# Sums' reciprocals spread by DMA and divided on GpSimd, a third norm by pairs of blocks with token-major scores, and combine weights turned eight tiles at once

## What is computed

```python
x = x + 0.5 * ffn(layernorm(x), ...)
x = x + attn(layernorm(x), ...)
x = x + 0.5 * ffn(layernorm(x), ...)
```

## Time and profile before

| | us |
|---|---|
| three runs | 1883.06, 1894.16, 1893.02 |
| median | 1893.02 |
| profiled execution | 1892.63 |
| its span | 1890.8 |
| mean granted TensorE clock | 0.965 of full |

### The profile page before, as it was taken

One profiled execution on the slowest core, in us unless ns is written; L12 is line 12 of the kernel. 1 busy time (PEld: TensorE's weight loads), 2 busy tenths in 40 slices (PEclk: granted clock), 3 DMA queues, 4 the chain that ended last, 5 costly groups with the idle time before them and its releaser, 6 DMA issues.

```text
span 1890.8 us, 38698 instructions
## 1 busy us (share of the span) xinstructions
PE 1764.9 (93%) x14955; PEld 754.2 (40%) x14955; DVE 1623.5 (86%) x1980; ACT 1468.3 (78%) x2741; POOL 371.9 (20%) x547
## 2 busy tenths in 40 slices
PE   5699998879999999999999999999999999699998
PEld 3488776712222222222222222222222223377786
DVE  6566775689999999999999999999999994476665
ACT  3455564719999999999999999999999996346455
POOL 4366551300000000000000000000000000155565
PEclk9899997859999999999999999999999998899999
DMA  4454330220000100000010000001000010523542
GB/s 117 93 129 125 105 105 1 100 85 9 32 20 22 33 24 21 26 32 20 22 34 23 22 26 31 20 22 35 22 22 27 30 28 3 107 91 111 104 137 78
DMA packets 66415, 98.90 MB, mean 52 GB/s; under 512 B 12091, under 2 KB 33408, under 8 KB 66212
## 3 DMA queue, kind: packets, MB, share of 16 engines
q1 hardware_dynamic: 62070, 94.32, 17.9%
q10 hardware_dynamic: 4160, 2.10, 0.4%
HBM read 84.94 MB, written 11.04 MB: 51 GB/s over the span
## 4 chain that ended last, share of the span: by engine, by line
PE 43%; ACT 27%; issue 4%; DVE 4%; DMA 1%; POOL 1%; SPq 0%; POOLq 0%; ACTq 0%; DVEq 0%
ACT at_prob L1158 26%; PE ps L1233 16%; PE ps L1221 15%; PE ps L615 3%; PE ps L633 3%; PE ps L623 3%; DVE at_mx L1268 2%; ACT at_sums L1163 1%; POOL e_part L688 1%; DMA e_cw<-comb_rows 1%; PE ps L1197 1%; PE ps L1354 0%; DVE ps L701 0%; PE ps L1369 0%; PE ps L1442 0%
## 5 line engine op out<-in xcount | busy, mean ns | idle before, releaser
L1268 DVE TENSOR_REDUCE at_mx<-ps 128x1 f32<-128x1024 f32 x1024 | 1169.4, 1216 | 12.4 <-PE ps L1197 12.4
L1158 ACT ACTIVATE at_prob<-ps 128x512 f32<-128x512 f32 x2048 | 1111.0, 595 | 71.9 <-PE ps L1221 51.8
L1233 PE MATMUL ps<-at_prob,vals 128*32 128x256 f32 x8192 | 656.3, 392 | 15.2 <-ACT at_sums L1163 15.2
L1197 PE MATMUL ps<-k_head,q_head 48*128 48x512 bf16 x2048 | 641.3, 389 | 12.1 <-PEq L801 7.8
L1221 PE MATMUL ps<-q_head,k_head 51*128 51x512 bf16 x2048 | 630.9, 383 | 4.9
L1233 PEld LDWEIGHTS ps<-at_prob,vals 128*32 128x32 f32 x8192 | 162.3, 108 | 430.1 <-ACT at_prob L1158 405.1
L688 POOL TENSOR_TENSOR e_part<-e_silu,e_cw 128x512 f32<-128x512 f32 (+1 forms) x208 | 268.0, 1289 | 269.5 <-ACT e_silu L659 122.9
L1221 PEld LDWEIGHTS ps<-q_head,k_head 51*128 51x128 bf16 x2048 | 130.1, 93 | 434.8 <-ACT at_prob L1158 402.9
L701 DVE TENSOR_TENSOR ps<-e_part,ps 128x512 f32<-128x512 f32 (+1 forms) x208 | 144.6, 695 | 155.9 <-POOL e_part L688 155.2
L659 ACT ACTIVATE e_silu<-ps 128x512 f32<-128x512 f32 (+1 forms) x208 | 124.4, 598 | 142.0 <-PE ps L615 140.1
L1092 POOL TENSOR_TENSOR at_mparts<-at_neg,at_zero 128x8 bf16<-128x8 f32 x64 | 12.9, 202 | 1104.9 <-DVE at_neg L1276 1104.9
(11 more groups left out here) (255 smaller groups left out, 1242.7 us busy)
## 6 DMA issues: line engine op xcount, KB each, us to landing
e_cw<-comb_rows SPq DMA_DIRECT2D x80, 256.0 KB, 3.3
e_cw<-comb_rows SPq DMA_DIRECT2D x32, 224.0 KB, 3.0
e_cw<-comb_rows SPq DMA_DIRECT2D x32, 192.0 KB, 3.1
q_head<-q_rows SPq DMA_DIRECT2D x64, 96.0 KB
k_head<-k_rows SPq DMA_DIRECT2D x64, 96.0 KB
e_cw<-comb_rows SPq DMA_DIRECT2D x32, 160.0 KB, 2.9
e_cw<-comb_rows SPq DMA_DIRECT2D x48, 96.0 KB, 2.8
e_cw<-comb_rows SPq DMA_DIRECT2D x32, 128.0 KB, 3.0
```

Source lines behind the costliest of these rows:

```text
L1158: act.activation(prob[:, t % PROBS, c, :], ps[:, S + n % SRING, :], ACT.Exp).then_inc(exped, 1)
L1197: made = pe.matmul(ps[:, M + 2 * (r % MRING) + one, :], q[h % BUFS][HALF:HALF + KR, tile * P:(tile + 1) * P], k[h % BUFS][HALF:HALF + KR, ...
L1233: done_one = pe.matmul(ps[32 * j:32 * j + 32, O, half * HALF_BLK:(half + 1) * HALF_BLK], vals[h % BUFS][:, g, :], prob[:, t % PROBS, j // ...
L1268: dve.tensor_reduce(mx[u % BUFS][:, j // 2, j % 2:j % 2 + 1], ps[:, at:at + 2, :].rearrange("p a t -> p (a t)"), AX.X, ALU.max).then_inc(m ...
```

## The change

**Reciprocals.** `block_rows`, the spreading matmuls and DVE's division are gone. The sums are handled in three groups of heads: 0 to 15, 16 to 27 and 28 to 31. For each, SP loads the denominators into as many partitions as fit (128x256, 96x256, 128x64) and the outputs, in one DMA, into `xnT_hi`, which is free then. DVE inverts, between reductions for the first two groups, after chunk 0's product in e3 for the third. SP stores the reciprocals to memory (`inv_rows`) and loads them back eight times over, one row for each channel, into `xnT_lo`. POOL multiplies outputs by reciprocals in SBUF: batch 0's four blocks after the splits of units 52 to 55, batch 1's after chunks 5, 7, 9 and 11 of e3.

**Norm.** Variances and powers are made for two blocks at a time (128x8 twice a batch instead of 128x16). Scores are token-major: the turned tile is the weight and 16 columns of gates move, 12 matmuls a block; ACT keeps them as logits directly.

**Combine weights.** Eight tiles of 128x9 are turned as one 128x72: two transposes and one copy a batch, stored by two DMAs. Batch 0's store stands ahead of the last head's sums in SP's queue.

**Places.** In the tail: projections at 1, 2, 4, 5 (with a wait for the last reductions, since they use banks of M), turns 10 to 13, scores 13 to 16, combine weights at 29. In e3: sums at 2, stores and loads of the reciprocals at 6 and 8, projections as before, variances and powers at 11 and 15, turns at 15, 19, 21, 25, routing by one stage a chunk at 31 and 33 to 41, combine weights turned at 42 and stored ahead of chunk 51.

```diff
-    def spread_out(self, pe, blk, bank, ring):
-        pe.wait_ge(self.inverted, blk // BPS + 1)
...
-        pe.matmul(self.ps[:, bank, :], self.block_rows[rows_of(blk), blk, :], self.inv[rows_of(blk), :],
-                  start=True, stop=True).then_inc(self.spread, 1)
-
-    def divide(self, dve, blk, bank):
...
-        dve.tensor_tensor(self.oT[:, blk % 2, :], self.o[:, blk % BPS, :], self.ps[:, bank, :],
-                          ALU.mult).then_inc(self.divided, 1)
+GROUPS = ((0, HEADS, 8), (HEADS, BH - LAST_HEADS, 8), (BH - LAST_HEADS, BH, 32))
+    def load_inverse(self, sp, g):
+        a, b, _ = GROUPS[g]
+        sp.wait_ge(self.inv_stored[g], 16)
+        sp.dma_start(self.rows(LO, g), self.inv_rows[a:b, :].bitcast(I32).unsqueeze(1).broadcast_to([b - a, HD, SEQ])).then_inc(self.inv_loaded[g], 16)
+
+    def divide(self, pool, blk):
+        for g in ((0,), (1, 2))[blk // BPS]:
+            pool.wait_ge(self.o_loaded[g], 16)
+            pool.wait_ge(self.inv_loaded[g], 16)
...
+        pool.tensor_tensor(self.oT[:, blk % BPS, :], self.sums_of(blk), self.factors_of(blk), ALU.mult).then_inc(self.divided, 1)
...
     def score(self, pe, blk, bank):
-        for n, (wp, xp) in enumerate(PASSES):
-            last = pe.matmul(self.ps[:, bank, :], self.gateT[wp][:], self.xnT[xp][:, blk * BLK:(blk + 1) * BLK],
+        for j in range(TPB):
...
+                last = pe.matmul(self.ps[:, bank, j * SCORE_COLS:(j + 1) * SCORE_COLS], self.xnT[xp][:, tokens],
+                                 self.gateT[wp][:, 0:SCORE_COLS], start=(n == 0), stop=(n == len(PASSES) - 1))
...
+    def attention_dve(self, dve, r, pairs):
+        if r == 43 * pairs + 8:
+            self.invert(dve, 0)
+        if r == 60 * pairs + 8:
+            self.invert(dve, 1)
...
+    SIDE_DIVIDES = (5, 7, 9, 11)
```

More of the change, by code:

```diff
@@ L1002 @@
 SUM_DMAS = BPS
[L1003 to L1012, removed]
+COMB_DMAS = 2
+COMB_TILES = NT // BATCH // COMB_DMAS
+SCORE_COLS = 16
+LAST_HEADS = 4
+GROUPS = ((0, HEADS, 8), (HEADS, BH - LAST_HEADS, 8), (BH - LAST_HEADS, BH, 32))
+DEN_COLS = (slice(0, 256), slice(256, 512), slice(512, 576))
+assert all((b - a) * m <= P and SEQ // m == c.stop - c.start for (a, b, m), c in zip(GROUPS, DEN_COLS))
 def attention_phase(nc, sem, kept, ps, v, identb, q, k, vals, q_rows, k_rows, qk_loaded, qk_stored,
@@ L1110, in _ @@
                     place(h - 2 + BUFS)
-            late.power(pool, 0)
+                late.attention_pool(pool, u)
+            for k in range(2):
+                late.power(pool, k)
         @block.sync
@@ L1379, in add, with vary @@
             last = dve.bn_stats(self.stats[:, j, :], self.x[:, j, :])
[L1380 to L1386, removed]
+        last.then_inc(self.counted, 1)
+    def vary(self, dve, k):
+        t = slice(2 * k * TPB, 2 * (k + 1) * TPB)
+        total, diff, within, mean, between, spread, var, _, _ = [self.small[:, i, t] for i in range(9)]
         even, odd = self.stats[:, t, 0:3], self.stats[:, t, 3:6]
-        at = b * (BPS + 7) + BPS
-        dve.wait_ge(self.step, at)
+        dve.wait_ge(self.counted, 2 * (k + 1))
         dve.tensor_tensor(total, even[:, :, 1], odd[:, :, 1], ALU.add).then_inc(self.step, 1)
@@ new lines, in attention_pool, with tail_pe @@
+    def attention_pool(self, pool, u):
+        if 52 <= u < 52 + BPS:
+            self.divide(pool, u - 52)
+    PROJECTS = (1, 2, 4, 5)
+    TAIL_TURNS = (10, 11, 12, 13)
+    TAIL_SCORES = (13, 14, 15, 16)
+    TAIL_COMB = 29
+    TAIL = TAIL_COMB + 1
+    def tail_pe(self, pe, at, M, max_reduced, steps):
+        for blk in range(BPS):
+            if at == self.PROJECTS[blk]:
+                pe.wait_ge(max_reduced, steps - 1 if blk < 2 else steps)
+                self.project(pe, blk, M + blk, BPS)
+            if at == self.TAIL_TURNS[blk]:
+                self.turn(pe, blk, M + blk, BPS)
+            if at == self.TAIL_SCORES[blk]:
+                self.score(pe, blk, M + blk)
+        if at == self.TAIL_COMB:
+            self.turn_comb(pe, 0, M)
@@ L1590, in tail_dve @@
+        self.normalize(dve, 3)
+        for blk in range(1, BPS):
+            self.keep_low(dve, blk, M + blk)
         for stage in range(10):
             self.route(dve, 0, stage)
[L1592 to L1597 removed]
+        self.keep_comb(dve, 0, M)
+    SIDE_DIVIDES = (5, 7, 9, 11)
+    SIDE_PROJECTS = (8, 10, 12, 14)
+    SIDE_VARIED = (11, 15)
+    SIDE_NORMS = (13, 17, 19, 23)
+    TURNS = (15, 19, 21, 25)
+    SIDE_COMB = 42
```

303 lines of the change are left out of this document (149 added, 154 removed).

## The result

The changed kernel takes 1880.27 us (median of 18 runs), the kernel before 1890.80 in as many: a ratio of 0.9941 (95% interval 0.9930 to 0.9952). It is faster, but by 0.6% where 1.5% was forecast: more than half of the gain is missing. The profiled execution of the changed kernel has a span of 1876.4 us.

The account below looks back on a forecast made before the run. The body was taken as bound by DVE's 1024 reductions, the tail by PE's order, e3's start by a chain, e3 by POOL's parts. 1892.6 - 13.8 (body and tail included) - 14.9 = 1863.9, given as 1864 us; range 1849 to 1882.

Parts of the forecast that it names:

- Body, +3.3: Attention body: two reciprocals of 1.67 us between DVE's reductions add their whole length, +3.3 us.
- Tail, -9.1: Tail, in PE's order: side work shrinks from 22.2 to 13.1 us, so the last scores come 9.1 us earlier.
- Start of e3, -13.8: Start of the second expert phase: first weight read at about 1614.5 instead of 1628.29, -13.8 us, reciprocals included.
- e3, -14.9: Second expert phase: -19.2 us of work and waits go, +2.8 and +1.5 come, sum -14.9.
- The reciprocals' wait: In e3, POOL's division after chunk 5 waits for the last group's inverses to be read back, +2.8 us (0 to 12).
- the load at the start: Early e3: POOL's 6.26 us wait for a weight load shrinks by 4.0 us, with 0.85 MB less queued.
- the additional powers with the divisions: In e3, POOL's four divisions and two additional powers, mostly covered by PE's lead, cost +1.5 us (0 to 6).
- The slow stretch: Early e3: the half-clock stretch behind POOL's load wait, costing one chunk 1.7 us, goes: -1.7.
- A: Rival, e3: inverses come late and stop POOL, so e3 gains 1.2 instead of 14.9; 1877 us, chance 0.18.
- B: Rival: inverses in time, body reciprocals hide in DVE's waits, the turns' loads overlap; 1854 us, chance 0.12.
- C: Rival, e3: new waits for inverses keep PE at half clock; 24 of 52 chunks cost 42 us, 1906; chance 0.05.
- D: Rival, e3's start: sum stores and barrier set it whatever routing does, gain 5.8 us; with A 1885; chance 0.05.

Follow-up runs that it names:

- 128 columns: Score matmuls move 128 columns of gates instead of 16, against the changed kernel; 1865.90 us, ratio 0.9866 to the kernel before.
- the six kernels whose tail runs at full clock: Follow-up variants of the changed kernel, all with tail scores 128 columns wide, some with a further edit; measured 1860.73 to 1880.84 us.

## Why the prediction was wrong

- **Body, +3.3: right.** Two reciprocals of 1.74 us, 3.3 us more in the second half, with DVE's waits unchanged.
- **Tail, -9.1: the step that failed.** The prices were right: with the clock at 1.00 (128 columns) the tail takes 40.9 us, 9.7 less than before. What failed is the clock. I read 0.116 us for a matmul of 16 columns off the qkv phase and took this price for the whole cost. I bounded half clock by 6 us, for scores and turns alone, as if the clock rose again behind them. (By my own factor of 1.8, that bound is 0.8 x 8.7 = 7 us.) The clock stayed at 0.50 to the end of the tail, and the steps behind the scores paid too. Of the 11.8 us that this cost, some 9.5 are eleven steps at 1.97 us instead of 1.11, and only some 2.4 are two groups of scores at 2.66 instead of 1.47.

Both parts of this could be read before the change. Three steps of the tail of the kernel before ran at half clock, at 1.97 us each, as from 1597.21 to 1599.18:

```profile
1597.21 1.03 PE L1221 MATMUL ps<-q_head,k_head 51*128 51x512 bf16 x2
1598.17 1.08 PE L1233 MATMUL ps<-at_prob,vals 128*32 128x256 f32 x8
1599.18 1.12 PE L1426 MATMUL ps<-ident,at_oT 128*128 128x128 f32 x4
```

And behind the 16 matmuls of the earlier trace rows, which end at 328.06, a window of the kernel before shows the lower level:

```profile
328.00:331.30 3.30, 3.17 (x9) 2.06 (x9) 2.35 (x5) 2.88 (x6) 0.00 (x0) 0.50 0.01 2
```

A pause of 1.39 us stands shortly ahead of those 16, so this row is a warning and not a proof.

- **Start of e3, -13.8: half right.** The link of routing and landing went as said, and the sums' stores stand in front of the first read. From the last scores to part 0 it took 14.2 us against 11.1. It is 12.4 to 14.3 in the six kernels whose tail runs at full clock. SP's stores begin 4.55 us behind the last scores, not 2.95 (3.1 with 128 columns, so this too is the half clock). The two stores of the weights take 1.38 us of SP, not 2 x 0.28, and the first read stands 10.0 us behind the last scores (8.5 at full clock), not 7.2.
- **e3, -14.9: the mechanism right, the size off by 4 us.** It gave 10.9. The border of the batches lost its waits as forecast. The reciprocals' wait was 2.15 us where I took 2.8 (2.2 to 5.7 in the other kernels whose first division stands at 5). Mis-sized were the load at the start, a wait of 5.18 us where I took 2.3, and the additional powers with the divisions, 1.5 us: one wait of 4.85 for DVE's variances stood in front of the second power, because POOL is called for it at the chunk at which DVE begins them. The slow stretch that I took as gone (-1.7) came again: the granted clock was 0.50 from 1640 to 1644. These do not add up to 4, since part of a wait of POOL is made up elsewhere. With 128 columns and the clock at 1.00 all through, the way took 128.8, by chance nearly the 128.4 of the forecast: the waits for the load (3.53 us), the reciprocals (3.28) and the variances (4.85) were there too.
- **Rivals.** The measured 1880 us lies inside my range and near A's 1877, but that is luck: A (late reciprocals) did not happen, and the range had no rival for what did. B is out: the reductions became longer by the reciprocals. C, half clock, named the right cause in the wrong stage: not e3's waits but the tail's scores. D is out: routing did stand on the path (4.9 us less from the last scores to part 0). The totals of A and B are 1877.6 and 1854.8 by their own terms.

What stays open is why the way from part 0 to part 52 varies with the same code in e3, by 3.7 us between profiles (128.8 to 132.5). The longer ones have the lower clock; what decides whether the clock dips there is not shown. Open, too, is what in the narrow matmuls brings the clock down in the tail: the runs show the two widths 16 and 128, and nothing between.

## What to carry to other kernels

In this kernel a matmul's price had two parts: its own time, and what it did to the clock of what followed. Before making matmuls narrower, look at what stands around them. In the tail here, between the matmuls of the attention's steps, the narrow scores left these at half clock to the end of the stage; in e3, between matmuls of 512 columns, they did not (the kernel that is wide in the tail only). Widening the moving side to columns that nobody reads cost next to nothing here (0.11 us a matmul either way), and it is a one-number test of that suspicion.

## What was not expected of the hardware

- By the profile PE was busy 10.00 of 10.00 us and the granted clock was 0.50. The Trainium skill, "TensorE: Matmul & The Clock Gate", Part 1: The HAM clock gate, explains the gate by how busy PE has recently been. The kernel with the doubled reciprocals agrees for a pause (2.88 us without work, then 0.50); the tail after the change doesn't: there was no pause, and only the width of the matmuls differed between 0.50 and 1.00.
- Steps with the same instructions ran at 1.00 ahead of the narrow scores (1.11 us) and at 0.50 behind them (1.97), for some 20 us: here they kept the level that they found. Before the change the clock rose again at about 1600, beside score matmuls of 512 columns.
- A matmul with 128 moving columns and a 128x128 weight tile of its own cost the same as one with 16: 0.11 us from start to start at full clock.
